# Rates on Sigmoid inside the first gate, and the last keys and queries scaled and turned between the gradients

## What is computed

```python
q = _l2_norm(q)
k = _l2_norm(k)
lr = jax.nn.softplus(x @ w_lr.T + BASE_LR_INV)
gate_before_act = w0 @ kT
hidden_before_mul = w2 @ kT
silu_gate = jax.nn.silu(gate_before_act)
hidden = silu_gate * hidden_before_mul
dhidden = jnp.swapaxes(w1, 1, 2) @ vT
dhidden_before_mul = dhidden * silu_gate
dgate = dhidden * hidden_before_mul
dgate_before_act = _silu_backprop(dgate, gate_before_act)
dw1 = vT @ (jnp.swapaxes(hidden, 1, 2) * lr1)
dw0 = dgate_before_act @ (k * lr0)
dw2 = dhidden_before_mul @ (k * lr2)
```

## Time and profile before

| what | value |
| --- | --- |
| median of 3 runs | 701.15 us (701.01 to 701.41) |
| profiled execution: time | 703.99 us |
| profiled execution: span | 702.2 us |
| PE busy | 660.0 us, 94% of the span |
| DVE busy | 481.3 us, 69% |
| ACT busy | 336.7 us, 48% |
| POOL busy | 218.6 us, 31% |

### The profile page before, as it was taken

How to read it: one execution, slowest core, us unless ns; L and a number is a source line. 1 busy time by engine, 2 the same in 40 slices (tenths; PEclk the granted TensorE clock), 3 DMA queues, 4 the chain that set the end, 5 groups by cost and what they waited for, 6 DMA issues and landing times.

```text
span 702.2 us, 11475 instructions
## 1 busy us (share of the span) xinstructions
PE 660.0 (94%) x4116; PEld 565.7 (81%) x4116; DVE 481.3 (69%) x953; ACT 336.7 (48%) x703; POOL 218.6 (31%) x212
## 2 busy tenths in 40 slices
PE   3989789789997899999999999999999999999997
PEld 3878679779996688788888888888888888888885
DVE  4598878999997588767546655576655666556545
ACT  3277679979995865543322322322332232232232
POOL 2267778858046573134001330023100330000000
PEclk9999999999998999999999999999999999999999
DMA  8120000021000000042102342233312332222123
GB/s 319 45 77 1 2 1 1 14 78 26 3 3 0 1 1 1 1 132 94 31 15 84 112 113 67 69 106 105 95 60 86 113 113 60 65 71 61 61 77 118
DMA packets 22568, 43.58 MB, mean 62 GB/s; under 512 B 3400, under 2 KB 5712, under 8 KB 22384
## 3 DMA queue, kind: packets, MB, share of 16 engines
q1 hardware_dynamic: 21488, 39.76, 18.4%
q10 hardware_dynamic: 832, 2.43, 1.0%
q0 software_dynamic: 192, 0.66, 0.2%
HBM read 40.60 MB, written 2.24 MB: 61 GB/s over the span
## 4 chain that ended last, share of the span: by engine, by line
PE 78%; DVE 8%; ACT 7%; POOL 3%; issue 2%; DMA 1%; ACTq 0%; DVEq 0%
PE ps L1021 38%; PE ps L1096 19%; PE ps L837 3%; PE ps L946 2%; PE ps L935 2%; PE ps L959 2%; PE ps L960 2%; PE ps L975 2%; DMA qkvw<-in_qkvw 1%; PE ps L1062 1%; PE ps L864 1%; ACT junk L699 1%; ACT junk L618 1%; PE ps L1042 1%; DVE x L1472 1%
## 5 line engine op out<-in xcount | busy, mean ns | idle before, releaser
L747 ACT ACTIVATE sgm<-ps,zero 128x512 f32<-128x512 f32 x100 | 68.9, 691 | 271.7 <-PE ps L1021 271.6
L1523 DVE TENSOR_TENSOR am<-sgm,ps 128x512 f32<-128x512 f32 x88 | 60.6, 689 | 139.7 <-ACT sgm L747 139.7
L1021 PE MATMUL ps<-h2hi,whi 128*128 128x512 f32 x400 | 156.1, 390 | 0.0
L1021 PE MATMUL ps<-h2lo,whi 128*128 128x512 f32 x400 | 155.6, 389 | 0.0
L1021 PE MATMUL ps<-h2hi,wlo 128*128 128x512 f32 x400 | 155.6, 389 | 0.0
L465 POOL CAST whi<-raw 128x768 fp32r<-128x768 f32 x25 | 22.7, 910 | 237.8 <-DMA raw<-in_moew 235.2
L1021 PEld LDWEIGHTS ps<-h2lo,whi 128*128 128x128 f32 x400 | 75.1, 188 | 15.7
L1021 PEld LDWEIGHTS ps<-h2hi,wlo 128*128 128x128 f32 x400 | 75.1, 188 | 15.4
L1021 PEld LDWEIGHTS ps<-h2hi,whi 128*128 128x128 f32 x400 | 75.1, 188 | 15.4
L1096 PE MATMUL ps<-ahi,whi 128*128 128x512 f32 x200 | 77.9, 390 | 0.1
L1096 PE MATMUL ps<-ahi,wlo 128*128 128x512 f32 x200 | 77.8, 389 | 0.0
(11 more groups left out here) (210 smaller groups left out, 1227.7 us busy)
## 6 DMA issues: line engine op xcount, KB each, us to landing
raw<-in_moew SPq DMA_DIRECT2D x25, 384.0 KB, 4.0
cw<-combine SPq DMA_DIRECT2D x32, 256.0 KB, 3.3
cw<-combine SPq DMA_DIRECT2D x16, 224.0 KB, 3.0
cw<-combine SPq DMA_DIRECT2D x16, 192.0 KB, 2.9
cw<-combine SPq DMA_DIRECT2D x16, 160.0 KB, 2.7
wog<-combine SPq DMA_DIRECT2D x2, 1024.0 KB, 6.6
cw<-combine SPq DMA_DIRECT2D x16, 128.0 KB, 2.9
out<-x1T SPq DMA_DIRECT2D x8, 256.0 KB, 3.0
```

What stands on the lines that cost most here:

```text
L747: ac.activation(sgm[:, n % 2, :], gate_bank(n), ACT.Silu, bias=zero[:, :]).then_inc(S["e_sg"], 1)
L1021: last = mm(o, w_, a_[:, kc, tok], start=(kc == 0 and k == 0), stop=(kc == KC - 1 and k == 2))
L1523: ve.tensor_tensor(am[:, n % 2, :], sgm[:, n % 2, :], lin_bank(n), ALU.mult).then_inc(S["e_a"], 1)
```

## The change

ACT's activation for the rates comes ahead of sigmoid(0) and is a Sigmoid of -|z| in place of an Exp; DVE's first step of the series turns from e + 2 into 2 - s, which with s = e/(1 + e) gives the same t. DVE's `through_gate` is split in two: `gate_slopes` (sg, u) and `gate_products` (hid, dhb). For batch 0 the series stands between them.

The last block's values are turned right behind the last queries of block 2, into banks 6 and 7. Block 2's queries are copied out by ACT (`turned_q`), and sigmoid(1) comes ahead of the rates' wait. The last block's norms stand on DVE behind batch 0's dgb, its keys are scaled on DVE behind batch 1's cast, its queries on POOL in two halves, behind the slopes of batches 1 and 2. PE turns its keys (banks 2, 3) just before fast_up(3) and its queries (banks 0, 1) just before fast_up(4). One head of each is copied out by ACT, the other by DVE (`last_turned` in either list), and fast_up(3) and fast_up(4), which write these banks, wait for both. grads waits for scaled keys head by head.

In the order of the lists POOL, ACT, PE, DVE (semaphores' names and unchanged lines left out):

```diff
+        def turn_ps(n):
+            blk, kind, h = n // 6, n % 6 // NH, n % NH
+            if blk < NBLK - 1:
+                return bank(2 + h)
+            return bank((6, 2, 0)[kind] + h)
...
+            def scale_q(blk, half_of=None):
+                po.wait_ge(S["nrm_ok"], 2 * (blk + 1))
+                first, n = (0, 4) if half_of is None else (2 * half_of, 2)
+                for t in range(blk * 4 + first, blk * 4 + first + n):
+                    q_t = qk[:, 0:NH, t, :]
+                    po.tensor_tensor(q_t, q_t, bc(rn[:, 0:NH, t:t + 1], P), ALU.mult).then_inc(S["sc_q"], 1)
...
-                po.wait_ge(S["nrm_ok"], 2 * (blk + 1))
-                for t in range(blk * 4, blk * 4 + 4):
-                    q_t = qk[:, 0:NH, t, :]
-                    po.tensor_tensor(q_t, q_t, bc(rn[:, 0:NH, t:t + 1], P), ALU.mult).then_inc(S["sc_q"], 1)
+                if blk < NBLK - 1:
+                    scale_q(blk)
...
-            po.wait_ge(S["sc_k"], NT)
+            po.wait_ge(S["sc_k"], NT - 4)
...
+                if b == (NBLK - 1) * 4 // TPB:
+                    po.wait_ge(S["sc_k"], NT)
...
+                if b in (1, 2):
+                    scale_q(NBLK - 1, b - 1)
...
-                    ac.activation(dst[:, h, blk * BLK:(blk + 1) * BLK], bank(2 + n % 2), ACT.Copy).then_inc(S["at_sb_a"], 1)
+                    ac.activation(dst[:, h, blk * BLK:(blk + 1) * BLK], turn_ps(n), ACT.Copy).then_inc(S["at_sb_a"], 1)
...
+            def turned_q(blk):
...
+                for h in range(NH):
+                    n = blk * 6 + 2 * NH + h
+                    ac.wait_ge(S["at_ps"], n + 1)
+                    ac.activation(qT[:, h, blk * BLK:(blk + 1) * BLK], turn_ps(n), ACT.Copy).then_inc(S["at_sb_q"], 1)
...
+            def last_turned(kind):
...
+                n = (NBLK - 1) * 6 + kind * NH
+                ac.wait_ge(S["at_ps"], n + 1)
+                ac.activation((vT, kT, qT)[kind][:, 0, (NBLK - 1) * BLK:], turn_ps(n), ACT.Copy).then_inc(S["at_sb_l"], 1)
...
-            for t in range(NT + 5):
+            for t in range(NT + 1):
...
-                if t == NT + 4:
-                    for h in range(NH):
-                        n = (NBLK - 1) * 6 + 2 * NH + h
-                        ac.wait_ge(S["at_ps"], n + 1)
-                        ac.activation(qT[:, h, (NBLK - 1) * BLK:], bank(2 + n % 2), ACT.Copy).then_inc(S["at_sb_v"], 1)
...
+                    ac.wait_ge(S["lr_z"], 2)
+                    ac.activation(lra[:, :, :], lra[:, :, :], ACT.Sigmoid, scale=-1.0, bias=zero[:, :]).then_inc(S["lr_e"], 1)
...
-                    ac.wait_ge(S["lr_z"], 2)
-                    ac.activation(lra[:, :, :], lra[:, :, :], ACT.Exp, scale=-1.0, bias=zero[:, :]).then_inc(S["lr_e"], 1)
+                    turned_q(NBLK - 2)
+                    turned_out(NBLK - 1, 0)
+                    sigmoid(1)
...
-                if b >= 1:
+                if b >= 2:
...
+                if b in (2, 3):
+                    last_turned(b - 1)
...
-                    elif kind == 0:
+                    elif kind == 0 and blk < NBLK - 1:
...
-                    else:
+                    elif kind == 1 and blk == NBLK - 1:
+                        pe_.wait_ge(S["b_dg"], 2)
+                    elif kind == 2 and blk == NBLK - 1:
+                        pe_.wait_ge(S["b_dg"], 3)
+                    elif kind:
...
-                        last = pe_.transpose(bank(2 + n % 2)[:, i * P:(i + 1) * P], src, ident[:, :])
+                        last = pe_.transpose(turn_ps(n)[:, i * P:(i + 1) * P], src, ident[:, :])
...
-                pe_.wait_ge(S["at_sb_a"], 2 * NH * (b * TPB // 4 + 1))
+                pe_.wait_ge(S["at_sb_a"], min(2 * NH * (b * TPB // 4 + 1), 2 * NH * (NBLK - 1) + NH))
...
-                    pe_.wait_ge(S["at_sb_v"], NH * NBLK)
-                    pe_.wait_ge(S["at_sb_a"], 2 * NH * NBLK)
+                    pe_.wait_ge(S["at_sb_q"], NH)
...
+                if b >= 3:
+                    pe_.wait_ge(S["at_sb_l"], min(b - 2, 2))
+                    pe_.wait_ge(S["at_sb_d"], min(b - 2, 2))
...
-            for t in range(NT + 5):
+            for t in range(NT + 1):
...
+            turned(NBLK - 1, 0)
...
-                pe_.wait_ge(S["b_kl"], 4 * (b + 1))
...
+                else:
+                    pe_.wait_ge(S["at_sb_a"], 2 * NH * (NBLK - 1) + NH)
...
+                    pe_.wait_ge(S["b_kl"], 4 * b + 2 * (h + 1))
...
+                if b in (3, 4):
+                    turned(NBLK - 1, b - 2)
...
+            def norms(blk, part):
...
+                tiles = slice(blk * 4, blk * 4 + 4)
+                n = 2 * blk + part + 1
+                heads = (slice(NH, 2 * NH), slice(0, NH))[part]
+                ve.wait_ge(S[("nrm_k", "nrm_q")[part]], blk + 1)
+                ve.tensor_scalar(qkn[:, heads, tiles], qkn[:, heads, tiles], L2_EPS, None, ALU.add).then_inc(S["nrm_e"], 1)
+                ve.wait_ge(S["nrm_e"], n)
+                ve.reciprocal(rn[:, heads, tiles], qkn[:, heads, tiles]).then_inc(S["nrm_ok"], 1)
...
+            def scaled_k(blk):
...
+                ve.wait_ge(S["nrm_ok"], 2 * blk + 1)
+                for t in range(blk * 4, blk * 4 + 4):
+                    k_t = qk[:, NH:2 * NH, t, :]
+                    ve.tensor_tensor(k_t, k_t, bc(rn[:, NH:2 * NH, t:t + 1], P), ALU.mult).then_inc(S["sc_k"], 1)
...
-                tiles = slice(blk * 4, blk * 4 + 4)
-                for i, (part, ready) in enumerate(((slice(NH, 2 * NH), "nrm_k"), (slice(0, NH), "nrm_q"))):
-                    n = 2 * blk + i + 1
-                    ve.wait_ge(S[ready], blk + 1)
-                    ve.tensor_scalar(qkn[:, part, tiles], qkn[:, part, tiles], L2_EPS, None, ALU.add).then_inc(S["nrm_e"], 1)
-                    ve.wait_ge(S["nrm_e"], n)
-                    ve.reciprocal(rn[:, part, tiles], qkn[:, part, tiles]).then_inc(S["nrm_ok"], 1)
-                    if i == 0:
-                        ve.wait_ge(S["nrm_ok"], n)
-                        for t in range(blk * 4, blk * 4 + 4):
-                            k_t = qk[:, NH:2 * NH, t, :]
-                            ve.tensor_tensor(k_t, k_t, bc(rn[:, NH:2 * NH, t:t + 1], P), ALU.mult).then_inc(S["sc_k"], 1)
+                norms(blk, 0)
+                scaled_k(blk)
+                norms(blk, 1)
...
-            def through_gate(b):
+            def gate_slopes(b):
...
+            def gate_products(b):
...
+                i = b % 2
...
-            scale_k(NBLK - 1)
-            q_out(NBLK - 2)
-            through_gate(0)
...
+            gate_slopes(0)
...
-            step(ve.tensor_scalar(lrp[:, :, :], lra[:, :, :], 2.0, None, ALU.add))
+            step(ve.tensor_scalar(lrp[:, :, :], lra[:, :, :], -1.0, 2.0, ALU.mult, ALU.add))
...
+            gate_products(0)
...
+            def last_turned(kind):
...
+                n = (NBLK - 1) * 6 + kind * NH + 1
+                ve.wait_ge(S["at_ps"], n + 1)
+                ve.tensor_copy((vT, kT, qT)[kind][:, 1, (NBLK - 1) * BLK:], turn_ps(n)).then_inc(S["at_sb_d"], 1)
...
-                    through_gate(b)
+                    gate_slopes(b)
+                    gate_products(b)
...
+                if b == 0:
+                    norms(NBLK - 1, 0)
+                    norms(NBLK - 1, 1)
...
+                if b == 1:
+                    scaled_k(NBLK - 1)
+                elif b in (2, 3):
+                    last_turned(b - 1)
```

More of the change, by code:

```diff
@@ L239, in build @@
             "stat1", "agg1", "var1", "rs_ok", "xn_ok", "tr_ps", "h1_ok", "h1_hi", "h1_lo", "qw_hi", "qw_lo",
-            "qkv_ps", "qk_sb", "v_sb", "sq_ok", "ss_ok", "nrm_k", "nrm_q", "nrm_e", "nrm_ok", "sc_k", "sc_q", "at_ps", "at_sb_a", "at_sb_v",
+            "qkv_ps", "qk_sb", "v_sb", "sq_ok", "ss_ok", "nrm_k", "nrm_q", "nrm_e", "nrm_ok", "sc_k", "sc_q", "at_ps", "at_sb_a", "at_sb_v", "at_sb_q", "at_sb_l", "at_sb_d",
             "lr_z", "lr_e", "lr_c", "lr_ok",
```

## The result

The changed kernel takes 712.67 us (median of 4 runs, 710.43 to 714.2) beside 701.28 us (701.01 to 704.45) of the kernel before: ratio 1.0141, 95% interval 1.0106 to 1.0176, so 7.4 to 12.3 us slower. Slower was forecast; 706.2 and the range up to 709.6 were too low. The profiled execution of the changed kernel took 710.43 us for a span of 708.6.

What follows compares the result with a forecast made beforehand. Bound by a serial chain with PE waiting (78 to 91 us), then a loop with PE and ACT full. Front -4.2, turns +4.6 and +3.75, clock +0.9: together +5.1 on 701.15, so 706.2 us, range 703.0 to 709.6.

Steps and rivals of the forecast that it cites:

- The front: Passage to the gradients: rates at about 84.6, grads(0) at 87.15 instead of 91.34, sigmoid(2) 4.2 us earlier (bounds 3.5 and 4.8).
- The two turns: Gradient loop, sigmoid(2) to sigmoid(4): fast_up waits for late copies; turns take 10.25 and 9.65, losing 4.6 and 3.75 us.
- DVE's lag: Turn 2 to 3: DVE's cast behind dgb(2) comes 0.2 to 2.0 us late from key products; 0.6 taken.
- the sum of the order: Start of sigmoid(4), clock aside: -4.2 + 4.6 + 3.75 = +4.2 us, bounds +2.95 to +6.25.
- The rival of hidden copies: fast_up(3) and fast_up(4) wait only for transposes, not squares: about 699 us, faster by 0.2 to 0.4%; chance 0.07.
- the swallowing tail: End of the loop: PE's 3.8 us wait absorbs the delay, end moves by 0.4, 701.6 us, no change; chance 0.08.
- the clock term: PE's gaps in passage and loop: one fall to half clock, 1.6 us, 0.6 hidden under DVE's lag, booked as +0.9 us.
- the clock at two or three gaps: Rival: PE's clock falls at two or three gaps, each 1.5 us, 707.2 to 710, say 708.5; chance 0.17.
- the forecast without the clock: From sigmoid(0): sigmoid(2) at 15.2, turns of 10.25 and 9.65, sigmoid(4) at 35.1, first step at 66.4 us.

Runs made afterwards that it cites:

- e10: e5 with the last block's keys scaled by ACT before sigmoid(1) instead of DVE's key products, their norms ahead of the first gate: 709.54 us, ratio 1.0094.
- e5: The changed kernel with 18, 15 and 11 extra identity products on PE in the gaps ahead of grads(0), fast_up(3) and fast_up(4): 709.0 us, ratio 1.0093.
- e9: The kernel before with 9 and 4 extra identity products on PE in the gap at the end of the loop: 702.57 us, ratio 0.9990.
- e3: The kernel before with the Sigmoid and the series between the gate's slopes and products, nothing turned elsewhere: 700.59 us, ratio 0.9982.
- e7: The kernel before with only the Sigmoid for the rates ahead of sigmoid(0), DVE's order left as it was: 701.33 us, ratio 1.0002.
- e8: e6 with 18 extra identity products on PE in the first gap, ahead of grads(0): 704.19 us, ratio 1.0011.
- e11: The changed kernel with last keys scaled and copied by ACT, turned in the first gap into banks 6 and 7, queries turned as in e6: 700.41 us, ratio 0.9980.
- e12: e11 with 9 extra identity products on PE ahead of grads(0): 699.74 us, ratio 0.9964.
- e6: The changed kernel with turnings between fast_up and grads, copies ahead of squares and dgb, key products ahead of the cast: 704.71 us, ratio 1.0010.

## Why the prediction was right and wrong

**The front was right.** The rates end 6.79 behind sigmoid(0) (82.61 - 75.82), forecast 7.1; grads(0) starts 9.36 behind it, 4.5 earlier than before, forecast 4.2. The Trainium skill (SBUF — State Buffer, "SBUF: two separate sides") gave 6.9, and the trace sides with it: the series' first step (0.20, from 77.94) was done about when POOL's u began, and the third, with two inputs (78.97, 0.52), ended just behind POOL's u (78.10, 1.27).

**The two turns were right in their path, and the match of the first is partly luck.** In e10 they measure 10.24 and 9.86 (forecast 10.25 and 9.65), with the releasers named: DVE's copies hold fast_up(3) and fast_up(4), ACT idles ahead of both sigmoids. But the 10.25 holds 0.6 of DVE's lag, and in e10 there is none, as the cast waits for ACT there (0.33). Cast and copy made up for it (1.54 from 99.48 to 101.02, where 1.21 was taken), and fast_up with its hand-over (3.04 for 2.8). So the sum of the order, +4.2 beside 4.25 in e10, is right to some 0.6 and no closer. The rival of hidden copies is out, and so is the swallowing tail: the +8.0 at sigmoid(4) is +8.7 at the first step.

**What failed is the clock term, "I count one fall", "+0.9".** Both the count and the size were wrong. The clock fell twice in the loop. grads(0) took 5.23 (85.18 to 90.41) instead of 2.9 in e5 (85.31 to 88.25): 2.3, outside the bounds of nothing and 1.6. The 1.6 came from grads(7), whose first products still ran at full clock (0.66 for the first group); grads(0) began behind a fall inside the gap and ran at half clock almost to its end. fast_up(3), to the sigmoid behind it, took 4.47 (100.42 to 104.89) instead of the 2.89 of fast_up(4) (111.87 to 114.76): 1.6. Together 3.9 against 0.9. (1.6 less the 0.6 hidden is 1.0, not 0.9; it changes nothing.) I had given this rival, the clock at two or three gaps, 0.17; it was the case that came, and at 708.5 it was too low as well. The Trainium skill (TensorE: Matmul & The Clock Gate, "HAM oscillation") describes a kernel in which each wait between bursts throws the clock back. Two of the three gaps here went that way (4.70 and 3.83); behind the shortest (3.23) the clock stayed at 1.00 from 112 to 116.

**The lag of DVE was mis-sized too, but it cost the changed kernel nothing.** 0.6 was taken, bounds 0 and 2.0. With the clock awake it measures 1.6 in e5, by the cast behind ACT's copies, and 1.4 of the turn goes with the key products (11.64 and, in e10, 10.24). In the changed kernel PE's slow products hide it; that the two hide under each other had been foreseen.

**The sum.** At sigmoid(4) the changed kernel is 8.0 late where 5.1 was forecast. Beside the forecast without the clock, sigmoid(2) makes 2.0 (2.3 for the clock, less the 0.3 by which grads(0) started earlier than forecast), turn 2 to 3 makes 1.6 (1.6 of the clock, 0.6 for a cast of 0.94 beside POOL and the hand-overs, less the 0.6 of lag), turn 3 to 4 makes 0.2: 3.8, of which 0.9 was booked. The tail adds 0.7: its clock, too, stood at 0.50, from 138 to 144, where e5 has 1.00 and gets from sigmoid(4) to the first step 1.4 sooner. The two medians differ by 11.4, the traces by 8.7 at the first step. Both lie in the interval of 7.4 to 12.3; the stage ahead of sigmoid(0) and the one behind the gradients vary by 4.9 and 2.9 us between the traces, in no order that goes with the change. What makes up the rest of the 11.4 is open.

## What to carry to other kernels

A wait that opens a gap on PE costs the gap and then the slow products behind it: price a fall by the whole length of the first group behind the gap (here 2.3 for the 24 matmuls that the profile counts in grads(0), not 1.6), and do not take one gap that passed without a fall as proof that the next of its length will. Costs that hide under each other aren't additive either way: taking away the clock's 4 brought out a lag that had been covered, and only taking away both gave 4.25. Before work is moved behind a full stage, look for the hole that the move itself opens: here the keys belonged into the gap of 4.7 us, on the engines that were waiting in it.

## What the hardware showed that I had not expected

The length of a gap alone does not sort the falls. Four traces have the same gap on PE, ahead of the transposes of the last values, the place of the first of the earlier trace rows. In the kernel before (2.72) and in e9 (2.68) the clock stayed at 1.00 behind it; in e3 (2.72) and e7 (2.66) it fell. A fall came behind 2.81 in e8, 3.46 ahead of grads(0) in e11, 3.83 ahead of fast_up(3) and 4.70 ahead of grads(0), and none behind 3.23 ahead of fast_up(4). The gap and the window behind it in e3, then the gap and windows of e7:

```profile
80.06 1.16 PE L793 MATMUL ps<-ident,v 128*128 128x128 f32 x8 [2.72 <-DVE qT L1162]
82.00:85.00 3.00, 2.87 (x13) 2.09 (x12) 2.76 (x8) 1.89 (x4) 1.54 (x2) 0.50 0.01 3
```

```profile
77.32 1.23 PE L793 MATMUL ps<-ident,v 128*128 128x128 f32 x8 [2.66 <-DVE qT L1162]
75.00:78.00 3.00, 0.68 (x6) 0.59 (x7) 2.97 (x9) 0.01 (x1) 2.23 (x4) 1.00 0.01 3
78.00:82.00 4.00, 3.82 (x20) 3.14 (x19) 3.86 (x8) 2.66 (x5) 2.80 (x3) 0.57 0.02 6
```

What decides between them stays open; no run here tells it. A fall that is prevented in one place came up in another: at 94 in e8, in the tail of e12 (0.66). And the same four key products of DVE took longer the more of POOL's products lay beside them: 1.43 with none, 2.26 with 1.3 us of them (the changed kernel), 2.68 with 2.1 (e5), 3.11 with 2.8 (e6).
